# Products that nobody reads in TensorE's holes, and scatters spaced by units, in a two-MoE-and-attention block on one core

## The reference

```python
x = x + 0.5 * ffn(layernorm(x))
x = x + attn(layernorm(x))
x = x + 0.5 * ffn(layernorm(x))

# ffn: 8 experts, 2 for each token
probs = softmax(flat @ gate_w.T)
weights, idx = top_k(probs, 2)            # then divided by their sum
h1 = einsum('nd,ehd->neh', flat, w1);  h3 = einsum('nd,ehd->neh', flat, w3)
y = einsum('neh,edh->ned', silu(h1) * h3, w2)
out = einsum('ned,ne->nd', y, combine)    # combine: the weights at the chosen experts
# attn: 16 heads of 8, causal mask, softmax, then @ WO
```

## Time and profile before

| | us |
|---|---|
| median of 3 runs | 622.59 (621.34 to 626.25) |
| profiled execution | 619.24 |
| its span, first to last instruction | 617.5 |
| TensorE busy, share of span | 84% |
| VectorE | 61% |
| ScalarE | 50% |
| GpSimd | 43% |
| mean granted clock of TensorE | 0.973 |

### The profile page before, as it was taken

One profiled execution on the slowest core, in us unless ns is written; L12 is line 12 of the kernel. 1 busy time (PEld: TensorE's weight loads), 2 busy tenths in 40 slices (PEclk: granted clock), 3 DMA queues, 4 the chain that ended last, 5 costly groups with the idle time before them and its releaser, 6 DMA issues.

```text
span 617.5 us, 19023 instructions
## 1 busy us (share of the span) xinstructions
PE 517.3 (84%) x7286; PEld 416.7 (67%) x7286; DVE 374.3 (61%) x995; ACT 310.2 (50%) x597; POOL 267.6 (43%) x325
## 2 busy tenths in 40 slices
PE   1779879999998578888888886777689899999995
PEld 1667858779987345555556564545368789989994
DVE  5633933333355778888989988666346343355665
ACT  4853524344334156666666765556553244345543
POOL 6865764630654033434342110554614530556562
PEclk9999988999998679999999999999989999999999
DMA  9941223546865222656212020311033546653232
GB/s 275 329 150 39 53 68 91 137 108 145 154 151 144 72 60 72 170 155 189 90 50 85 16 88 2 115 36 37 31 74 93 144 124 122 152 131 99 66 90 56
DMA packets 114662, 65.87 MB, mean 107 GB/s; under 512 B 51856, under 2 KB 108432, under 8 KB 114576
## 3 DMA queue, kind: packets, MB, share of 16 engines
q1 hardware_dynamic: 107664, 50.49, 31.1%
q0 software_dynamic: 6912, 14.17, 8.6%
HBM read 18.88 MB, written 34.87 MB: 87 GB/s over the span
## 4 chain that ended last, share of the span: by engine, by line
PE 37%; DVE 16%; issue 4%; ACT 3%; another core or an unknown queue 1%; DMA 1%; POOL 0%; DVEq 0%; ACTq 0%; POOLq 0%
PE bank L1621 9%; DVE negmax L1302 7%; PE bank L1502 5%; PE bank L1504 5%; PE bank L1503 5%; PE bank L1734 2%; PE bank L1797 2%; ACT pt L950 2%; PE bank L1764 2%; PE bank L1812 1%; PE bank L1751 1%; PE bank L1800 1%; DVE rden L1319 1%; PE bank L1514 1%
## 5 line engine op out<-in xcount | busy, mean ns | idle before, releaser
L1189 DVE SCALAR_TENSOR_TENSOR pt<-bank,pt 128x512 f32<-128x512 f32 x122 | 84.3, 691 | 154.5 <-PE bank L1504 72.6
L694 POOL DMA_INDIRECT yg<-sorted_y,row x108 | 104.3, 965 | 145.8 <-PE bank L1621 65.7
L950 ACT ACTIVATE pt<-bank 128x768 f32<-128x768 f32 x128 | 103.8, 811 | 88.0 <-PE bank L1773 83.1
L680 POOL DMA_INDIRECT sorted_x<-xs,row x108 | 106.2, 983 | 78.9 <-DVE pt L1189 33.0
L1621 PE MATMUL bank<-w,pt 128*128 (+1 forms) x976 | 133.1, 279 | 8.5 <-issue 7.3
L1621 PEld LDWEIGHTS bank<-w,pt 128*128 128x128 f32 x976 | 120.5, 193 | 14.1 <-issue 10.0
L1302 DVE TENSOR_REDUCE negmax<-bank 128x10 f32<-128x640 f32 x128 | 104.2, 818 | 30.2 <-PE bank L1751 26.4
L833 ACT ACTIVATE pt<-bank 128x512 f32<-128x512 f32 x122 | 73.2, 600 | 50.0 <-PE bank L1504 37.3
L841 ACT ACTIVATE yb<-bank 128x256 f32<-128x256 f32 x82 | 31.5, 384 | 76.6 <-PE bank L1621 50.7
L1734 PE MATMUL bank<-zc 63*64 63x64 f16 (+3 forms) x1024 | 44.1, 250 | 30.4 <-DVE negmax L1302 24.8
L1734 PEld LDWEIGHTS bank<-zc 63*64 63x64 f16 x1024 | 19.3, 107 | 58.1 <-DVE negmax L1302 38.7
(11 more groups left out here) (171 smaller groups left out, 1022.6 us busy)
## 6 DMA issues: line engine op xcount, KB each, us to landing
sorted_y<-yb SPq DMA_DIRECT2D x82, 128.0 KB
zc<-qk_rows SPq DMA_DIRECT2D x96, 64.0 KB
sorted_x<-zeros SPq DMA_DIRECT2D x2, 2944.0 KB, 14.1
qk_rows<-qksplit SPq DMA_DIRECT2D x8, 512.0 KB
sorted_x<-zeros SPq DMA_DIRECT2D x1, 2432.0 KB, 11.5
sorted_x<-zeros SPq DMA_DIRECT2D x1, 2176.0 KB, 10.2
X<-x_in SPq DMA_DIRECT2D x8, 256.0 KB, 5.1
zc<-w_up SPq DMA_DIRECT2D x8, 256.0 KB, 6.1
```

What stands on the lines that cost most here:

```text
L680: ps.indirect_dma_start(out=sorted_x[s], out_offset=bass.IndirectOffsetOnAxis(ap=row[:, s, k, t:t + 1], axis=0), in_=xs[:, R0[s] + t, :], ...
L694: ps.indirect_dma_start(out=yg[:, a % D_YG, k, :], out_offset=None, in_=sorted_y[s], in_offset=bass.IndirectOffsetOnAxis(ap=row[:, s, k, t ...
L950: s_.activation(pt[:, hg, (u % 2) * 768:(u % 2 + 1) * 768].rearrange("p (a n) -> p a n", a=2), bank[:, B_ST:B_ST + 2, 0:384], ACT.Exp, sca ...
L1189: v_.scalar_tensor_tensor(hid[:, n % D_HID], bank[:, B_H3 + n % 2, :], 1.0 / WSCALE, silu[:, n % D_H], ALU.mult, ALU.mult).then_inc(prod_d ...
```

## The change

Two things. First, a helper `keep_warm(n, b0)` on TensorE issues n products of `zeros` by `zeros`, 256 columns each in 16 bits, into a PSUM bank that holds nothing at that time; they signal nothing and nobody reads them. It is called in the head (64 before the first transposes, as soon as `zeros` is written; 6 ahead of the transposes of each of groups 1 to 7; 32 ahead of `sums(0)`; 10 behind the first `block_parts`) and in the prologue (3 behind each of 8 pairs, 5 behind each of 4 pairs): 192 products. Second, the scatters of set 1 (n from 24) wait for product 11 + 13(n-24)/20, rounded down, and those of set 3 for product `U_TILE[2]` + 3 + 7d/10.

```diff
@@ first_pace, GpSimd
-                if n >= FREE:
+                if n >= 2 * RT[0]:
+                    pool.wait_ge(prod_done, done(2 * BLOCKS[0] + 7 + (n - 2 * RT[0]) * 13 // 20, D_H))
+                elif n >= FREE:
                     pool.wait_ge(prod_done, done((n - FREE) * 7 // 10, D_H))
@@ scatters of set 3, GpSimd
-                pool.wait_ge(prod_done, done(U_TILE[2] + LAG + 6 * d // 10, D_H))
+                pool.wait_ge(prod_done, done(U_TILE[2] + LAG + 7 * d // 10, D_H))
@@ TensorE
+            def keep_warm(n, b0):
+
+                for _ in range(n):
+                    t_.matmul(bank[:, b0, 0:2 * D], zeros[:, 0:D], zeros[:, :], start=True, stop=True)
+
...
+            pe.wait_ge(consts, 1)
+            keep_warm(64, B_Y[0])
             pe.wait_ge(consts, 6)
             pe.wait_ge(w_lo, 1)
             transpose_first(0)
             for g in range(1, GROUPS):
                 if g == 5:
+                    keep_warm(32, B_Y[0])
                     pe.wait_ge(consts, 15)
                     sums(0)
+                keep_warm(6, B_Y[0])
                 transpose_first(g)
                 gate_first(g - 1)
                 if g >= 6:
                     block_parts(0, g - 6)
+                if g == 6:
+                    keep_warm(10, B_Y[0])
...
             for k in range(PAIRS):
                 score_products(0, 0, k, 0, score_banks(k), 1)
                 score_masks(score_banks(k))
+                keep_warm(3, B_O)
             for k in range(AHEAD):
                 score_products(1, 1, k, None, score_banks(k), 1)
                 score_masks(score_banks(k))
+                keep_warm(5, B_O)
```

## The result

The change does not make the kernel faster; it makes it a little slower. Measured side by side, the median after is 628.97 us (13 runs, 623.86 to 631.48), before 623.08 us (13 runs, 621.34 to 626.25): a ratio of 1.0067 [1.0045, 1.0088]. The forecast was 611.6 us, faster by more than 1%, range 604 to 619. The profiled execution took 627.51 us.

The account below looks back on a forecast made before the run. Bounds: TensorE's low clock and signals delayed by scatter trains, VectorE in the prologue. Head 4.5, set 1 pacing 3.5, set 3 1.0, prologue 2.0 sum to 11.0 us; 619.24 less that, plus 3.35, gives 611.6 us, range 604 to 619.

Parts of the forecast that it names:

- The six ahead of each transpose: Head, up to 25 us: six dummy products take 0.65 us per group, hidden because ScalarE sets the pace of 2.68 us.
- The 32: Head, ahead of `sums(0)`: 3.5 us at the high level, inside TensorE's 4.33 us wait for `chosen`; 6.8 us at low.
- the clock falls between the groups: Rival, head: each six costs 1.28 us, sums come 5.3 us late, head gains zero; total 616.1 us; chance 0.15.
- Slower: Rival: clock falls and the 32 do not restore it; decided if TensorE reaches them after 25.5 us; 633.3 us; chance 0.10.
- the first rival: The rival in which the clock falls between the head's groups; head zero, total 616.1 us; chance 0.15.
- the 6.1 us saved behind it: Head, behind the 32: savings of 1.5, 3.8 and 0.8 us from work, units and last gates at the high level.
- The head's ceiling and floor: Bounds on the gain from the head's dummy products: ceiling 8.4 us, floor 2.5 us, 4.5 us taken.
- Pacing: Later scatters in the experts' parts break the trains that delay units: set 1 gains 3.5 us, set 3 gains 1.0 us.
- pacing gives nothing: Rival, experts' parts: scatters keep forming groups and the unit rate stays; total 616.1 us; chance 0.25.
- Prologue: Attention's prologue: dummy products hide under VectorE's row maxima and the high level saves 2.0 us, bounds 0 and 2.5.
- if the level holds: Prologue's condition: with the high level kept, the 3.4 us from 219.65 to 223.06 us halve.
- The sign: Whole kernel: faster, 11.0 us saved; probabilities faster 0.70, same 0.20, slower 0.10.

Follow-up runs that it names:

- e11: The head's 148 dummy products alone, six ahead of each transpose, added to the kernel before; 620.70 us, ratio 1.0023 [0.9986, 1.0059].
- e16: The whole changed kernel measured once more against the kernel before; 573.49 us, ratio 1.0042 [1.0019, 1.0064].
- e6: Kernel before plus the head's dummy products, twelve instead of six ahead of each transpose; 567.43 us, ratio 0.9938 [0.9917, 0.9958].
- e10: Kernel before plus head products with twelves and prologue products with 22 behind the last pair, no new pacing; 616.62 us, ratio 0.9971 [0.9936, 1.0007].
- e12: Kernel before plus the head's dummy products with twelves, same edit as e6 in a slower series; 617.78 us, ratio 0.9999 [0.9965, 1.0033].
- e15: Same kernel as e10 (twelves in the head, 22 in the prologue, no new pacing), faster series; 566.38 us, ratio 0.9909 [0.9884, 0.9934] to before.
- e13: Kernel before plus only the 32 dummy products ahead of `sums(0)`; 620.75 us, ratio 1.0056 [1.0019, 1.0092].
- series 2: One of five sets of runs, each with its own measurement of the kernel before; a faster one, where before took 570.55 us.
- e9: Kernel before without the second scatter of every tile of sets 0 and 1, 28 scatters fewer; 600.86 us, ratio 0.9726 [0.9658, 0.9794].
- e8: Kernel before plus the prologue's dummy products, with 22 instead of five behind the last pair; 567.85 us, ratio 0.9960 [0.9938, 0.9982].
- e1: Kernel before plus only the head's 148 dummy products, sixes ahead of the transposes; 627.73 us, ratio 1.0090 [1.0056, 1.0123].
- series 1: One of five sets of runs, each with its own measurement of the kernel before; a slower one, where before took 623.50 us.
- before_look: The unchanged kernel before, run once for its trace in a slower series, where before's median was 619.20 us.

## Why the prediction was wrong, point by point

**The step that failed first** is "The six ahead of each transpose take 0.65 us ... so they cost nothing there". It assumed that what the 64 had raised would stay raised. Six 256-column products a round did not keep the level: it fell between 15.3 us (e11) and 20.8 us (e16) in all six traces that have them, each six then cost 1.44 us, and the round 3.65 us against ScalarE's 2.68. Twelve kept it through these groups in all four traces that have them (e6, e10, e12, e15). My argument against that rival, that the six fill a quarter of each period, was a share without a measured bound; the trace of before held only the opposite evidence, a full row at the low level.

**The 32.** "3.5 us at the high level, inside the 4.33 us hole" was right as arithmetic (3.65 us in e12) and wrong in place: they ran 6.52 us from 26.93 us and `sums(0)` slipped 4.3 us. The rival "the clock falls between the groups" had nearly these numbers (round 3.8 us, sums 5.3 us late, the clock back behind the 32). TensorE reached the 32 at 26.9 us, past the 25.5 us that the rival "Slower" gave as its mark. The total of the first rival was too kind: it let the 6.1 us saved behind it cancel the slip. They were not saved. The level fell again at 43.1 us, amid the products of unit 0 (TensorE had waited 0.47 and 0.49 us near 40 and 41 us; why it fell is not shown), so the next units ran as slowly as before, and the scatters, later by 4.1 us (36.84 against 32.75), then met the units in a train of fifteen.

**The head's ceiling and floor.** The text named both things that were to happen, the gate signal that "still comes 1.4 us after a train" and the longer train, and then took 4.5 us, nearer the middle. Its floor of 2.5 us assumed that two units would still shorten. They did not: in e12 the signal came 1.6 us behind the train, TensorE idled 4.92 us, and the level fell ahead of units 1 and 2, so 1.1 us came at product 0 and none at product 2. e13 gave 5.6 us at product 0 and minus 1.8 at product 2. The floor should have been below nothing. Where trains do not hold TensorE back (series 2) the term was 3.9 us at product 2, near the 4.5 forecast; that the total there agrees with it is in part luck, since the traces have only 0.4 us of it left at product 57.

**Pacing.** The mechanism was right locally: the train broke after five, units 13 to 17 took 13.6 us and not 16.7 (10 to 11 were forecast). The size was wrong: for set 1 3.5 us were forecast and 1.0018 [0.9978, 1.0059] measured, which excludes it; for set 3 1.0 us was forecast and 1.0003 [0.9972, 1.0035] measured, which tells it neither from nothing nor from the forecast. The forecast priced a unit under groups of five at 0.45 us and one under the train of ten at 2.0, from rows of one trace, and had no term for what stands behind the scatters on GpSimd: the wait for `rstd`, 4.2 us with the new pace and 0 to 2.1 without. Fewer scatters gave 21.6 us (e9), the same scatters spaced gave nothing. The rival "pacing gives nothing" is what happened.

**Prologue.** The dummy products stayed hidden under VectorE (eight maxima in 6.10 us, 6.06 before) and raised the level, as said. The failing step is "if the level holds": between the last scores and the loop TensorE waits 1.97 us for the maxima, the level fell there at 217.2 us, and all of what was to be halved ran at the low level (20.8 us from the first maximum, 205.63 us, to the slot at 226.40; 20.3 before). TensorE's rows after:

```profile
217.86 0.48 PE L1747 MATMUL bank<-zc 63*64 63x64 f16 x8 [1.97 <-DVE negmax L1304]
...
226.40 0.48 PE L1747 MATMUL bank<-zc 63*64 63x64 f16 x8
```

With the hole bridged and the level held the term was 1.7 us in e8 and 2.0 us in e10, forecast 2.0: right in size, once its condition was met.

**The sign.** Forecast 11.0 us saved; the profiled execution lost 8.3 us (627.51 less 619.24), the medians 5.9. The head alone loses that much in e1; in e11 it loses 1.4 us, and the interval includes none. Why e1 lost 0.9% in one series and e11 0.2% in another, where before differs by 5 us, is open; so is why the prologue's edit as made cost 0.5% in series 1, although its local distance is 20.15 us and thus no longer than before. That the four edits gain nothing as made is shown; how the loss of 5.9 us is shared out among them is not.

## What to carry to other kernels

Products that keep the clock up have to be shown to keep it up in every hole on their way: here six a round did not, twelve did, and a wait of 4.92 us behind them undid it all the same. Where they fail they run at the low level on the path. Ahead of pricing what an earlier step saves, look at what it lets start and at the next wait: here an earlier first unit lengthened a train of transfers, and VectorE's wait for `rstd` took back most of a gain of 4.5 us. Ahead of spacing instructions on an engine, look at what stands behind them in its order. And leaving out half of the transfers gave time where spacing them gave none; e9 is no usable program, it shows only how much hangs on their number.

## What the runs showed of the hardware

One kernel takes 571 us in some series and 619 to 623 us in others, and the difference stands where indirect transfers from GpSimd run: 2.2 us a unit under a train in e6, 3.3 and 4.1 us in e12. Attention shows it too. Three times eight slots without such a transfer take 42.8 us in before_look (330.06 to 372.86 us) and 42.6 us in e6 (302.90 to 345.54 us); the 24 slots behind them, with 19 transfers, take 51.6 and 43.5 us. In a slower series TensorE issued one product in 0.73 us at the end of a train (55.78, 56.51, 57.24 us of the changed kernel), and 28 scatters left out gave 21.6 us. The granted clock fell to 0.50 in 20 to 30 us with TensorE busy for 10.00 of 10.00 us, on rounds of six 256-column products, four transposes and eight 8-column products; with twelve in place of six it stayed at 1.00.
